# Jump sizes turned by a matmul, page arithmetic put first, third chunk of pages held back

## What is computed

```
x = x + L0(x)      # a linear layer whose 512x512 weight is quantized to a codebook
x = x + L1(x)      # attention over a paged cache

# L0
cb = codebook / max|codebook|;  thresholds = (cb[:-1] + cb[1:]) / 2
normalized = (weight + lora_delta) / exp(scale_log)
quantized  = cb[searchsorted(thresholds, normalized)]
w_eff = quantized * scale + lora_delta

# L1: 64 sequences, 32 query heads, 8 key heads of 128, block_table (64, 16) of pages
kc = k_cache[block_table]; vc = v_cache[block_table]      # 64 pages of 32 tokens
scores = q @ [kc, k].T, masked by cache_seqlens; softmax; @ [vc, v]; @ Wo
```

## Time and profile before

| | us |
|---|---|
| median of 3 runs | 2225.23 (2221.85 to 2225.42) |
| the profiled execution's own time | 2227.97 |
| its span, first to last instruction | 2226.2 |
| first block, from the span's start | 182.6 |
| VectorE busy over the span | 1717.5 (77%) |
| TensorE busy over the span | 2127.7 (96%) |
| mean granted TensorE clock | 0.987 |

### The profile page before, as it was taken

The page is one execution under the profiler, slowest core; times in us unless marked ns, Lnnn a source line. Parts: engine busy times, 40 slices in busy tenths (PEclk is TensorE's granted clock), DMA queues, the critical chain, the costliest instruction groups (busy, mean ns, idle before and its releaser), DMA issues.

```text
span 2226.2 us, 60848 instructions
## 1 busy us (share of the span) xinstructions
PE 2127.7 (96%) x17868; PEld 1394.2 (63%) x17868; DVE 1717.5 (77%) x3918; ACT 1474.0 (66%) x4950; POOL 1275.9 (57%) x2086
## 2 busy tenths in 40 slices
PE   5667989999999999999999999999999999999998
PEld 2324556666666666666666666666666666666665
DVE  7885668777777777777777777777778777777785
ACT  4633567776767777776766666677767666666664
POOL 3852135555556656656656666666665656566663
PEclk9998999999999999999999999999999999999999
DMA  7777567667666666677669567656656665666563
GB/s 219 263 274 228 188 180 217 205 198 210 195 202 205 189 206 202 189 214 207 196 203 290 178 211 227 177 176 187 175 170 182 188 181 173 184 180 180 174 182 101
DMA packets 479047, 440.15 MB, mean 198 GB/s; under 512 B 53101, under 2 KB 407740, under 8 KB 477950
## 3 DMA queue, kind: packets, MB, share of 16 engines
q1 hardware_dynamic: 433278, 295.70, 45.0%
q0 software_dynamic: 40960, 134.25, 19.6%
q10 hardware_dynamic: 4480, 6.29, 1.0%
HBM read 377.24 MB, written 56.70 MB: 195 GB/s over the span
## 4 chain that ended last, share of the span: by engine, by line
PE 84%; DVE 1%; SPq 1%; issue 0%; DMA 0%; ACT 0%; another core or an unknown queue 0%; DVEq 0%; ACTq 0%
PE PR L1309 21%; PE Op L1290 15%; PE WOp L1348 15%; PE Sp L1256 14%; PE PTp L1267 11%; PE TRp L1322 3%; PE Sp L1259 2%; PE Op L1272 1%; PE Op L1292 1%; PE TRp L1333 1%; SPq L740 0%; DVE masked L1500 0%; DMA wsrc<-in_L_cond_Wo 0%; DVE pts L1505 0%; PE WOp L1333 0%
## 5 line engine op out<-in xcount | busy, mean ns | idle before, releaser
L721 POOL DMA_INDIRECT pages<-values_split,rows x512 | 515.2, 1006 | 104.0 <-issue 85.7
L1309 PE MATMUL PR<-Wt,xT 128*128 128x512 f16 x2232 | 539.0, 380 | 0.0
L1399 ACT ACTIVATE pts<-PTp 128x512 f16<-128x512 f32 x512 | 306.6, 599 | 344.8 <-PE PTp L1267 275.5
L1290 PEld LDWEIGHTS Op<-pts,pages 128*128 128x128 f16 x6144 | 385.2, 98 | 122.7 <-DVE OT L1518 5.7
L1290 PE MATMUL Op<-pts,pages 128*128 128x128 f16 x6144 | 426.7, 219 | 3.4 <-DVE OT L1518 3.3
L1500 DVE CUSTOM_DVE_ANT_0 masked<-Sp,mask 128x544 f32<-128x544 f32 x512 | 369.7, 722 | 77.8 <-PE Sp L1259 44.8
L1256 PE MATMUL Sp<-pages,qT 128*128 128x512 f16 x1536 | 416.4, 380 | 6.9 <-PEq L186 6.8
L1405 ACT ACTIVATE masked<-masked,small 128x544 f32<-128x544 f32 x512 | 380.1, 742 | 42.6 <-DVE small L1500 37.0
L1505 DVE TENSOR_TENSOR pts<-PTp,pts 128x512 f16<-128x512 f32 x512 | 350.9, 685 | 70.2 <-ACT pts L1399 44.2
L1348 PE MATMUL WOp<-WoT,OT 128*128 128x512 f16 x1536 | 377.5, 379 | 0.0
L1518 DVE TENSOR_TENSOR OT<-Op,OT 128x128 f16<-128x128 f32 x512 | 148.0, 289 | 245.4 <-ACT p L1393 161.8
(11 more groups left out here) (246 smaller groups left out, 3021.7 us busy)
## 6 DMA issues: line engine op xcount, KB each, us to landing
pages<-keys_transposed SPq DMA_DIRECT2D x2048, 64.0 KB
mask<-mask_rows SPq DMA_DIRECT2D x128, 128.0 KB
v<-new_values SPq DMA_DIRECT2D x96, 128.0 KB
weights_split<-wdst SPq DMA_DIRECT2D x40, 256.0 KB
keys_transposed<-pages SPq DMA_DIRECT2D x32, 256.0 KB, 6.0
values_split<-pages SPq DMA_DIRECT2D x16, 512.0 KB, 5.1
rope_s<-rope_table SPq DMA_DIRECT2D x32, 256.0 KB
pages<-values_split,rows POOLq DMA_INDIRECT x512
```

Of the source, the lines that this page charges most:

```text
L721: nc.gpsimd.indirect_dma_start(out=vS[:, n % 2, c, :, :].rearrange("p l n -> p (l n)"), out_offset=None, in_=v_d, in_offset=bass.IndirectO ...
L1290: nc.tensor.matmul(o, vS[:, par, c, low, h * D:(h + 1) * D], pts[:, u % 2, part, c * P:(c + 1) * P], start=(k == 0), stop=False)
L1309: m = nc.tensor.matmul(bank(k), xT[:, c, xl, :], Wp[:, c, wl, GROUP_COL[k]:GROUP_COL[k] + HID], start=(i == 0), stop=(i == NPASS - 1))
L1399: nc.scalar.activation(pts[:, u % 2, 0, :], PTp[:, :], ACT.Copy).then_inc(G.pt_hi, 1)
```

## The change

- The jump row's trip through DRAM is gone. TensorE makes the row with one float32 product: the jump column, broadcast, by the identity (`jump_turned`), put behind the four LoRA products and ahead of `turn(0)`. VectorE copies from that PSUM bank.
- SP loads the raw block table ahead of `load(1)`; ahead of `load(2)` it now waits for `norm_done_first`.
- GpSimd does both parts of the page table ahead of `values_low(0)`.
- VectorE does six angle steps (instead of four) ahead of step 0, and the other two behind steps 1 and 3.

```diff
                 sp.dma_start(seq_col, seqlens.rearrange("(n o) -> n o", o=1)).then_inc(G.mask_table, 16)
+                sp.dma_start(bt_raw, page_list.to_broadcast([P, B * NPP])).then_inc(G.pages_loaded, 16)
                 load(1)
-                sp.wait_ge(G.sq_done, 1)
-                sp.dma_start(jump_d[0:NCB - 1]..., tiny[0:63, 8:9]).then_inc(G.jump_moved, 16)
-                sp.wait_ge(G.jump_moved, 16)
-                sp.dma_start(jump[:, 0:NCB - 1], jump_d[0:NCB - 1]...to_broadcast([P, NCB - 1])).then_inc(G.jump_moved, 16)
+                sp.wait_ge(G.norm_done_first, 1)
                 load(2)
-                sp.dma_start(bt_raw, page_list.to_broadcast([P, B * NPP])).then_inc(G.pages_loaded, 16)
...
                     nc.tensor.matmul(PR[:, c % 2, :], lBT[:, c * P:(c + 1) * P], lA, start=True, stop=True).then_inc(G.deltas, 1)
+                pe.wait_ge(G.sq_done, 1)
+                nc.tensor.matmul(TRp[:, 0:NCB], tiny[0:63, 8:9].to_broadcast([63, P]), ident[0:63, 0:NCB], start=True, stop=True).then_inc(G.jump_turned, 1)
                 turn(0)
...
-                v.wait_ge(G.jump_moved, 32)
-                V.tensor_copy(jump2[0:64, :], jump[0:64, 0:64:2])
-                link(V.tensor_copy(jump2[64:128, :], jump[64:128, 1:64:2]))
+                v.wait_ge(G.jump_turned, 1)
+                V.tensor_copy(jump2[0:64, :], TRp[0:64, 0:NCB:2])
+                link(V.tensor_copy(jump2[64:128, :], TRp[64:128, 1:NCB:2]))
...
-                for step in range(4):
+                for step in range(6):
                     angles(step)
...
-                    if step in (1, 3, 5, 7):
-                        angles(4 + step // 2)
+                    if step in (1, 3):
+                        angles(6 + step // 2)
...
+                g.wait_ge(G.pages_loaded, 16)
+                for part in range(2):
+                    page_table(part)
                 for c in range(NC):
                     values_low(c)
-                    if c == 3:
-                        g.wait_ge(G.pages_loaded, 16)
-                    if c in (3, 8):
-                        page_table((c - 3) // 5)
```

More of the change, by code:

```diff
@@ L82, in build @@
     rope_d = nc.dram_tensor("rope_table", (TILES, P, ROPE), F32).ap()
-    jump_d = nc.dram_tensor("jump_row", (NCB,), F32).ap()
     page_d = nc.dram_tensor("page_numbers", (HALVES * B * NPP,), I32).ap()
@@ L158, in build @@
         block_sems = {n: sem(n) for n in (
-            "loaded", "codebook_loaded", "tables_loaded", "positions", "angles", "abs_done", "trig_done", "table_part", "table_done", "bank_summed", "weff_turned", "weff_hi", "weff_lo", "const_done", "chain_v", "chain_g", "chain_a", "pe_done", "evac_hi", "evac_lo", "jump_moved", "x_first", "stage_first", "stage_loaded_0", "stage_loaded_1",
+            "loaded", "codebook_loaded", "tables_loaded", "positions", "angles", "abs_done", "trig_done", "table_part", "table_done", "bank_summed", "weff_turned", "weff_hi", "weff_lo", "const_done", "chain_v", "chain_g", "chain_a", "pe_done", "evac_hi", "evac_lo", "jump_turned", "x_first", "stage_first", "stage_loaded_0", "stage_loaded_1",
             "table_loaded", "wsrc_loaded_0", "wsrc_loaded_1", "w_turned", "w_hi", "w_lo", "w_stored", "wo_part",
@@ L303, in _ @@
                 sp.dma_start(seq_col, seqlens.rearrange("(n o) -> n o", o=1)).then_inc(G.mask_table, 16)
+                sp.dma_start(bt_raw, page_list.to_broadcast([P, B * NPP])).then_inc(G.pages_loaded, 16)
                 load(1)
-                sp.wait_ge(G.sq_done, 1)
-                sp.dma_start(jump_d[0:NCB - 1].rearrange("(n o) -> n o", o=1), tiny[0:63, 8:9]).then_inc(G.jump_moved, 16)
-                sp.wait_ge(G.jump_moved, 16)
-                sp.dma_start(jump[:, 0:NCB - 1], jump_d[0:NCB - 1].rearrange("(o n) -> o n", o=1).to_broadcast([P, NCB - 1])).then_inc(G.jump_moved, 16)
+                sp.wait_ge(G.norm_done_first, 1)
                 load(2)
-                sp.dma_start(bt_raw, page_list.to_broadcast([P, B * NPP])).then_inc(G.pages_loaded, 16)
                 for c in range(NC):
@@ L536, in _ @@
                 V.memset(n5[:, :, :], 0.0)
-                V.memset(jump[:, 63:64], 0.0)
                 V.memset(thr[:, 63:64], BIG)
```

## The result

| | before | after |
|---|---|---|
| median, us (9 runs each) | 2223.94 (2221.85 to 2225.42) | 2217.68 (2215.21 to 2218.21) |
| the profiled execution: time, span | 2227.97, 2226.2 | 2217.8, 2216.0 |
| step 0 starts | 33.02 | 32.32 |
| VectorE's stalls on TensorE | 7.35, 3.19, 0.21 | 11.83 |
| last step ends | 162.17 | 158.12 |

The ratio of the changed kernel to the one before is 0.997, 95% interval 0.996 to 0.9981: faster by 6.3 us, 0.3% (0.2 to 0.4). The profiled execution of the kernel before, 2227.97 us, lies above all nine of its runs in this table, so the two profiles do not differ by the change alone; the last experiment comes back to that. The forecast was 2219.5 with a range of 2215.0 to 2227.5, and faster with a chance of 0.56.

What follows compares the result with a forecast made beforehand. VectorE was taken to bound the first block; -6.5 + 3.1 - 4.2 + 1.9 = -5.7 us took the profiled 2227.97 to 2222.2, and runs' median lying 2.7 lower gave 2219.5 us, range 2215.0 to 2227.5.

Steps and rivals of the forecast that it cites:

- step 0 after 31, waiting for the pairing: Sign of being wrong: VectorE's step 0 starts after 31 us because the paired rows' DMAs land late; forecast start 28.8.
- Jump trip: Ahead of step 0: DRAM trip removed, step 0 4.2 us earlier, two angle steps (2.3) no longer between steps; -6.5 us.
- One stall instead of two: Ahead of step 11: page table before values delays load(3); one VectorE stall of 13.9 us instead of 10.8; +3.1 us.
- Less stretching: First block: page instructions lengthen VectorE's instructions by 3.2 us in all instead of 7.4; -4.2 us.
- values: First block: twelve values_low instead of eleven stretch a VectorE instruction; +1.9 us, bounds 0 and +3.7.
- The first rival: Nothing measurable: two-operand angle steps keep GpSimd out, 3 page instructions instead of 7 by 28.8; gain 2.0, 2223.2 us; chance 0.32.
- slower: Page instructions are as long with VectorE idle, so the one stall exceeds those replaced; 2231.9 or 2228.8 us; chance 0.12.
- The third: Rival: the jump row waits because TensorE reaches its product late; at most a us; chance less than 1 in 50.
- The fourth: Rival: page table through by 46.9 us, VectorE resumes at 57.5; gain 9, 2216 us; included in the forecast's 0.56.

Runs made afterwards that it cites:

- the last experiment: The kernel before and the changed kernel, both unchanged, profiled a second time on one chip: 2229.46 and 2223.51 us (1 run each).
- the page half: Kernel before with only the block table's load and the page table moved, jump row still through DRAM: 2214.57 us, ratio 0.9952; repeated 2221.00, 0.9962.
- the run with one wait more: Changed kernel with VectorE also waiting for the paired rows ahead of its six angle steps: 2222.18 us, ratio 0.9965 to the kernel before.
- the spread table: Changed kernel with values_low(0) first, then the page table's first part, its second by twos behind values_low(2) to (8): 2212.48 us, ratio 0.9941; repeated 2216.89, 0.9940.
- the first set: One chip's runs: jump row change alone, page table move alone, changed kernel without load(2)'s wait, and page table spread out; kernel before's median there 2224.20 us.

## Why the prediction was right, and where it was not

The forecast was a gain of 5.7 us; the medians show 6.3, and the barrier of the profiled pair 4.0. The chain of the argument held: VectorE is the bound of the first block, the two stalls go, one comes ahead of step 11, it is ended by TensorE waiting for chunk 3, whose load waits for the end of the page table. That the total came so near to the medians is in part luck. The sum speaks of the first block, where it was 1.7 us too high: two terms were off by 3.5 and 2.0 us, in opposite directions. What the medians gained beyond that block it did not foresee. One of the prediction's own signs of being wrong came true, "step 0 after 31, waiting for the pairing"; and step 10 ended at 50.47 (said: near 47), the stall was 11.83 (12 to 16), the last step ended at 158.12 (near 156) and the barrier was 178.62 (near 177). Term by term:

1. *Jump trip, -6.5.* It was **-3.0**. The row is there at once, as said, but step 0 started at 32.32 and not at 28.8. The mis-sized part is the new wait: the paired rows were in at 32.3, outside the 27.4 to 31 that I gave. `load(2)` goes out at the same time as the four pairing DMAs; without it beside them step 0 was at 30.5, inside the bounds, so 1.8 of the 3.5 us are `load(2)`'s. The six angle steps, 21.47 to 29.28, took 7.8 us and not 6.1, since page instructions stretched each of them, but that lies inside the same wait and cost nothing.
2. *One stall instead of two, +3.1.* It was **+1.1**: 11.83 against 10.75. The two ends were both late, step 10 ending at 50.5 (said: 46.9) and the page table at 51.6 (50.3). The remaining 8.48 + 2.12 us of the chain were right to 0.1. The two errors of the first two terms are one and the same: while VectorE waits longer for its rows GpSimd gets further. At 28.8 it had done 7 instructions, as I had taken; but step 0 came 3.5 us later, and at 32.8 all 13 of the first part were through. So a later step 0 is paid back in a shorter stall. The run without the hold on `load(2)` shows the trade directly, 1.8 us earlier, 2.3 us longer.
3. *Less stretching, -4.2, and values, +1.9.* Twelve `values_low` stretch an instruction of VectorE's and the last waits behind the steps, as said. From the start of step 0 to the end of step 10 are 18.15 us, where the forecast, 12 stretches included, has 18.1 (46.9 - 28.8); from the end of the stall to the last step's end are 95.8, where it has 95.4. So both terms were right: with them as forecast the sum is -3.0 + 1.1 - 4.2 + 1.9 = -4.2, against 4.05 measured at the last step.

Two readings of the prediction were off and cost it little. It took 0.24 us for what an L705 really holds and the rest of its 1.42 for waiting, and 0.34 for its length beside an idle VectorE. With VectorE idle such an instruction takes 0.48 to 0.49 (L702 at 29.73 to 30.89; eight in a row 4.50 in the page half), so the stretch of a step is half its own length, and less of the 1.42 is waiting. And it took a lock that lasts for a whole two-operand instruction to leave only two borders in the six angle steps, where such a lock by itself leaves the border between two of them open.

The first rival's condition did not come true. Ahead of L504, L506 and L508, with two operands each, a page instruction got in every time (1.39 us each instead of 1.22); ahead of L512 at 39.30 it did not, as with the 2.39 us of the earlier trace rows. The L702 beside L504 to L508 took 1.33 us each, against 0.48 alone. So two operands do keep GpSimd out for the length of the instruction, as the Trainium skill ("SBUF — State Buffer", Who interferes with whom) has it, and the trace agrees. What decides whether GpSimd gets in at the border in front is argued, not shown. In the rows, each of L504, L506 and L508 needs the result of the instruction just ahead of it, and there is a gap of 0.03 us; the run with one wait more has the same three at 1.39 to 1.40. L512's predecessor was long done, and there is no gap. But without a gap GpSimd got in at times too: ahead of the kernel before's L527 at 119.86 (1.62 us) and not ahead of its like at 107.99, 111.90 and 115.82. The rival "slower" needed a page instruction that is as long with VectorE idle as beside it; L703 at 31.46 and L704 at 51.01, 0.62 and 0.61 us, decide against it. The third, a jump row that waits, did not come true either: VectorE is not idle ahead of its copies. The fourth, more than forecast, had 12 page instructions in by 28.8 and the table through when step 10 ends; 7 were in by then, and the table was through at 51.62, 1.15 us behind step 10.

What the sum did not see is as large as its errors: removing the trip was in part bad. I took the 7.98 us of the earlier trace rows as lost, and costed what the page table needs as if it were independent of it. The page half alone is 3 us faster than the whole, and the spread table 7: what would have been the better change is not among the rivals.

## What to carry to other kernels

Where two engines take turns, the idle time of one is working time of the other: before removing a wait of VectorE's, ask what GpSimd does in that time, and cost both changes together. Work that only has to be done by the end of a stage, as an index table, goes in small pieces between the urgent instructions of its queue, not in one piece ahead of them. And where an engine's instruction has two lengths in the trace, find one that ran with the other engine idle; that is its own length, the rest is waiting. Compare profiles only within one chip, and look at the stretches that the change does not touch: here one of them, the block behind the barrier, differed by 3 to 4 us between chips, nearly as much as the change was worth.

## What was not expected of the hardware

- One more wait on VectorE, 10.87 us in place of 3.04, brought the barrier 2.3 us forward (176.94 against 179.21 in the same set).
- A page instruction on GpSimd takes 0.48 us (32x128) or 0.61 (128x512) with VectorE idle, 1.33 to 1.5 beside its instructions, and costs a step of VectorE's only 0.24 or 0.36.
- GpSimd got in ahead of each of L504, L506 and L508, where VectorE has a gap of 0.03 us (1.39 us each instead of 1.22, in two runs); without a gap it got in ahead of one of five two-operand instructions beside the page table (L527 at 119.86, not L512 at 39.30 nor the three at 107.99, 111.90 and 115.82).
- The same block, from the barrier to the last addition of x, took 91.3 to 91.9 us in the five profiles of the first set and of the changed kernel's first run, and 94.2 to 95.9 in the seven of the other two sets (95.1 in the kernel before's first). SP's 16 key loads behind the barrier took 8.11 to 8.12 us to issue in those five, and 10.70 to 12.01 in the other eight.
